# Two maxima of a head pair back to back in a two-layer decoder stage

## The reference, cut to what matters

```
def _mha(q_in, k_in, v_in, Wq, Wk, Wv, bv, causal):
    q, k = einsum(q_in, Wq), einsum(k_in, Wk)
    v = einsum(v_in, Wv) + bv
    scores = einsum('bhse,bhte->bhst', q, k) * HEAD ** -0.5     # 16 heads of 16
    if causal: scores = where(tril, scores, -inf)
    return einsum('bhst,bhte->bhse', softmax(scores), v)        # heads side by side
sa = _mha(x, x, x, Wq1, Wk1, Wv1, bv1, causal=True)
x = _layernorm(sa + x, g1, be1)
ca = _mha(x, enc, enc, Wq2, Wk2, Wv2, bv2, causal=False)
x = _layernorm(x + ca, g2, be2)
```

## Time and profile before

| what | value |
|---|---|
| median of 3 runs | 1558.11 us (1557.0 to 1561.98) |
| the profiled execution | 1571.12 us, its span 1569.4 us |
| mean granted TensorE clock | 0.859 |
| PE busy | 1153.9 us (74%) |
| VectorE busy | 975.9 us (62%) |
| ScalarE busy | 613.1 us (39%) |
| GpSimd busy | 463.6 us (30%) |

### The profile page before, as it was taken

One profiled execution on the slowest core, in us unless ns is written; L12 is line 12 of the kernel. 1 busy time (PEld: TensorE's weight loads), 2 busy tenths in 40 slices (PEclk: granted clock), 3 DMA queues, 4 the chain that ended last, 5 costly groups with the idle time before them and its releaser, 6 DMA issues. The chain is left out here.

```text
span 1569.4 us, 26159 instructions
## 1 busy us (share of the span) xinstructions
PE 1153.9 (74%) x9362; PEld 767.7 (49%) x9362; DVE 975.9 (62%) x2633; ACT 613.1 (39%) x1214; POOL 463.6 (30%) x616
## 2 busy tenths in 40 slices
PE   2687767777499710788888888820599997699998
PEld 1364444444278610677777777720254543345454
DVE  4645566777247530788888888834465652477776
ACT  1334455666355201566566656500154443000000
POOL 4234554323426644133333333355110100100000
PEclk9777898999789855899999999965586876799999
DMA  6323222322023234565666556245121210101000
GB/s 187 106 58 98 68 86 83 124 79 62 20 82 117 92 120 177 212 234 211 206 231 239 202 208 233 72 129 174 56 59 46 74 31 28 55 27 34 26 9 14
DMA packets 130245, 171.35 MB, mean 109 GB/s; under 512 B 13747, under 2 KB 104646, under 8 KB 127174
## 3 DMA queue, kind: packets, MB, share of 16 engines
q1 hardware_dynamic: 126534, 160.77, 31.3%
q0 software_dynamic: 3584, 8.92, 1.8%
HBM read 123.31 MB, written 46.14 MB: 108 GB/s over the span
## 5 line engine op out<-in xcount | busy, mean ns | idle before, releaser
L1972 PE MATMUL moe_ps_u<-moe_x_hl,moe_up_hl 128*128 128x256 f16 x1932 | 226.5, 276 | 68.8 <-DVE moe_up_hl L2048 42.6
L1972 PEld LDWEIGHTS moe_ps_u<-moe_x_hl,moe_up_hl 128*128 128x128 f16 x1932 | 184.5, 99 | 110.8 <-DVE moe_up_hl L2048 49.1
L2335 PE MATMUL mix_ps_e<-wr_hl,mix_u_hl 128*128 128x512 f16 x768 | 172.4, 380 | 0.0
L2092 POOL CAST moe_mid_hl<-moe_mid 128x256 f16<-128x256 f32 x161 | 71.8, 446 | 291.8 <-DVE moe_mid L2063 291.8
L2048 DVE SCALAR_TENSOR_TENSOR moe_up_hl<-moe_up_in,moe_up_hl 128x512 f16<-128x512 f32 x161 | 123.3, 799 | 54.4 <-ACT moe_up_hl L2021 54.4
L542 ACT ACTIVATE dec_probs<-dec_ps_t 128x768 f32<-128x768 f32 (+1 forms) x128 | 117.2, 917 | 83.3 <-PE dec_ps_t L444 83.1
L2447 DVE SCALAR_TENSOR_TENSOR mix_acc<-mix_ps_e,mix_shares,mix_acc 128x256 f32<-128x256 f32 x256 | 110.3, 477 | 39.0 <-PE mix_ps_e L2335 38.7
L1294 DVE TENSOR_REDUCE memory_neg_m<-memory_ps_s 128x2 f32<-128x512 f32 x128 | 84.8, 689 | 66.2 <-PE memory_ps_s L1071 63.5
L2021 ACT ACTIVATE moe_up_hl<-moe_up_in 128x512 f16<-128x512 f32 x161 | 99.2, 619 | 62.0 <-DMA moe_up_in<-in_moe_w 62.0
L431 PE MATMUL dec_ps_s<-dec_k_st,dec_q_st 48*128 48x256 f16 (+1 forms) x512 | 51.5, 281 | 90.6 <-DVE dec_neg_m L640 47.1
L2335 PEld LDWEIGHTS mix_ps_e<-wr_hl,mix_u_hl 128*128 128x128 f16 x768 | 74.8, 98 | 83.4 <-issue 1.1
(11 more groups left out here) (278 smaller groups left out, 2101.1 us busy)
## 6 DMA issues: line engine op xcount, KB each, us to landing
moe_up_in<-in_moe_w SPq DMA_DIRECT2D x23, 1792.0 KB, 7.6
moe_down_in<-in_moe_w SPq DMA_DIRECT2D x23, 896.0 KB, 4.7
moe_raw<-in_mix_wr SPq DMA_DIRECT2D x32, 256.0 KB, 7.7
dec_q_dram<-dec_q_hl SPq DMA_DIRECT2D x48, 128.0 KB, 2.0
dec_k_dram<-dec_k_hl SPq DMA_DIRECT2D x48, 128.0 KB, 2.0
dec_q_st<-dec_q_dram SPq DMA_DIRECT2D x64, 96.0 KB, 2.5
dec_k_st<-dec_k_dram SPq DMA_DIRECT2D x64, 96.0 KB, 2.6
xs<-zeros SPq DMA_DIRECT2D x8, 736.0 KB
```

What stands on the lines that cost most here:

```text
L1972: mm = nc.tensor.matmul(bank[:, m, :], up_hl[t.slot][:, w, m, dc, f * P:(f + 1) * P], x_hl[t.slot][:, x, dc, :], start=(dc == 0 and w == x ...
L2335: mm = nc.tensor.matmul(ps_e[fill % RING][:, :, :], u_hl[t.slot][:, r, dc, k * P:(k + 1) * P], wr_hl[:, m, dc, 2 * q:2 * q + 2, :], start= ...
```

## The change

Within an eighth VectorE does both maxima first and everything else behind them. Some other calls are moved by an eighth with it: the low part of QUERY from eighth 2 to 1, the low part of KEY from 3 to 2, the divisions from 3 and 7 to 2 and 6. No instruction is added or taken away, no wait is changed, and the loops of the other engines stay.

```
                 for t in STEPS:
                     nxt, new, old, older = t + 1, t + 2, t - 1, t - 2
                     for p in range(PAIRS):
+                        if within(nxt):
+                            maximum(nxt, 2 * p)
+                            maximum(nxt, 2 * p + 1)
+                        if p == 0 and within(new):
+                            rows_low(new)
+                        if p == 1 and within(new):
+                            projected_low(new, QUERY, q_hl)
                         if p == 2 and within(new):
-                            projected_low(new, QUERY, q_hl)
-                        if p in (3, 7) and within(old):
+                            projected_low(new, KEY, k_hl)
+                        if p in (2, 6) and within(old):
                             divide(old, p // 4)
                         if p == 1 and within(older):
                             statistics(older)
                         if p == 4 and within(older):
                             normalise(older)
-                        if within(nxt):
-                            maximum(nxt, 2 * p)
-                        if p == 0 and within(new):
-                            rows_low(new)
-                        if p == 3 and within(new):
-                            projected_low(new, KEY, k_hl)
-                        if within(nxt):
-                            maximum(nxt, 2 * p + 1)
```

## The result

| | before | after |
|---|---|---|
| median of 4 runs | 1557.55 us (1556.51 to 1561.98) | 1540.04 us (1532.74 to 1541.24) |
| the profiled execution, its span | 1571.12, 1569.4 us | 1541.24, 1539.5 us |
| mean granted clock | 0.859 | 0.874 |
| PE / VectorE busy | 1153.9 / 975.9 us | 1139.3 / 975.2 us |

The ratio is 0.9872, interval [0.9836, 0.9909]. The forecast of 1549.0 had the direction, and its range held the time, because case 2 had set the lower edge; the gain is about twice the 9.1 us of the sum (17.5 by the medians), and lies in the interval of case 2, which I had given 0.22.

A forecast was written before the change was run, and what follows sets the result against it. The prediction took the decoder stage to be held by handovers between engines, with no engine full. Its terms, -19.0 + 13.3 - 3.4 = -9.1 us, took the median from 1558.11 to 1549.0; its 8-in-10 range was 1539.5 to 1555.

The forecast's parts named there:

- case 2: Filled hole ahead of QUERY also keeps the clock up: half to all of 9.5 us more, 1539.5 to 1544.3; chance 0.22.
- the sum: Decoder schedule: -19.0 (head) + 13.3 (later division) - 3.4 (normalisation) = -9.1 us, with the clock's effect taken as zero.
- Eighths 0 and 1: Head of the decoder step: rows_low behind maximum 1 starts QUERY 1.36 us earlier, 19.0 us over 14 steps.
- case 4: No change to be told: scores 1, not rows_low, set QUERY's start, so the head gives less; 1557.2 us, chance 0.10.
- Eighths 2 and 3: Division behind KEY's low part loses its cover: scores 4 come 1.00 us later a step, 13.3 us lost in all.
- The statistics: Moved behind QUERY's low part, their 0.94 us on VectorE cost nothing, since later maxima wait for the division anyway.
- The normalisation: Moved behind maximum 9, its collision with GpSimd's context split is hidden in four steps: 3.4 us gained.
- Case 3: The normalisation still holds VectorE where it counts: 3.4 us less gain, 1552.4 us; chance 0.10.
- The clock: Granted clock in decoder steps 0 to 8: taken as zero, between 9.5 us gained at QUERY and falls of 2.13 each.
- if QUERY and VALUE take other times than now: Sign in the trace after that would show the forecast wrong: changed durations of these decoder projections.
- Case 5: Slower: new hole ahead of the first values drops the clock there and at VALUE; eight falls, 1566.0 us; chance 0.08.

The follow-up runs named there:

- e7_norm_back: Changed kernel with the normalisation put back ahead of maximum 8; 1555.25 us, ratio 0.9891 to the kernel before.
- e2_key_ahead: Kernel before with only the low part of KEY moved ahead of the first division; 1578.74 us, ratio 1.0140 to the kernel before.
- e1_head_only: Kernel before with only rows_low moved behind maximum 1; 1541.68 us, ratio 0.9823 to the kernel before.
- e4_hole_back: Changed kernel with one wait added: PE waits for rows_low ahead of scores 1; 1558.14 us, ratio 0.9989 to the kernel before.
- e6_swap: Changed kernel with the division ahead of the low part of KEY in eighth 2; 1547.94 us, ratio 0.9835 to the kernel before.

## Why the prediction was wrong in its size

**Eighths 0 and 1: right.** -1.36 forecast, -1.45 measured (3.51 to 2.06). The order is the one drawn: maximum 1, scores 1, rows_low, then QUERY. This also refutes case 4: QUERY waits for rows_low (0.55 us) and not for scores 1.

**Eighths 2 and 3: right.** +1.00 forecast, +0.91 measured (5.45 to 6.36). The product ends a little earlier, and the first values fit in as computed, from 288.98 to 290.05, under scores 4 at 290.17. PE's new wait ahead of them is 0.87 there.

**The statistics: right.** At 285.15, maxima 4 and 5 behind them, ended at 287.35, and the low part of KEY at 287.52 waits 0.17 for ScalarE.

**The normalisation: right in size, wrong in its cause.** Scores 4 to scores 5 take 1.72 us in a step where they took 2.60, in order of time:

```profile
139.59 0.34 PE L431 MATMUL dec_ps_s<-dec_k_st,dec_q_st 48*128 48x128 f16 x4 [0.25 <-DVE dec_neg_m L640]
...
140.37 1.16 POOL L743 TENSOR_TENSOR context<-dec_ctx_raw,context 128x512 f16<-128x512 f32 x1 [1.31 <-ACT context L533]
...
141.08 1.23 DVE L669 TENSOR_SCALAR dec_total<-dec_total,dec_mv,dec_rstd 128x256 f32<-128x256 f32 x2
141.31 0.50 PE L431 MATMUL dec_ps_s<-dec_k_st,dec_q_st 48*128 48x128 f16 x4 [0.84 <-DVE dec_neg_m L640]
```

The pair meets the end of the split (1.23 instead of 0.73), hidden. But e7_norm_back and e2_key_ahead are free of the collision with the normalisation at its old place: the later division shifts the split, a step that I had not followed as far as GpSimd. Case 3, in which the normalisation still costs its 3.4 us, fails with it.

**The schedule in sum: nearly right.** Re-measured it is 14 x 1.45 = 20.3 less, 13 x 0.91 + 0.2 = 12.0 more and 3.4 less: -11.7 where I had -9.1.

**The clock: the step that failed.** "In steps 0 to 8 the granted clock falls and rises ... I take zero." It was worth -8.6 at QUERY, against a bound of 9.5 that stood in the text. KEY gave back 0.3 (1.26 us above full clock instead of 0.94), and VALUE, which I feared for, gave 0.8 (5.6 instead of 6.4). With these the sum is -20.8, of the 22.5 by which this decoder ended earlier. The sign that the prediction itself had set, "if QUERY and VALUE take other times than now", was met. In the second pair of executions QUERY gives 7.7 and VALUE 0.2, and yet the decoder ends only 13.0 earlier; what took the rest there is open.

What shows the cause is e1_head_only, by one move, together with where the clock falls in all traces; e4_hole_back shows that one wait undoes the gain at QUERY, and leaves open how. What misled me was the argument against case 2: "the steps at full clock have the same hole of 2.3 us before scores 1 and no fall." (The hole is 2.09 there.) That a hole is met without a fall in some steps shows that it isn't enough by itself; it doesn't show that it isn't needed. With 2.04 to 2.09 us of idleness ahead of all nine QUERYs that were long, these should have weighed more than the steps without a fall. The two kinds of step also differ in what stands ahead: in steps 3 to 8 PE idled another 0.9 to 1.3 us ahead of the values that stand before the turned rows, in 9 to 13 it did not. No run tests that, and in the second execution of before QUERY was long in step 9, without it.

**Case 5: a true fall, too small.** e2_key_ahead shows what the move does alone: four VALUEs of the cross layer at 2.56 to 2.66, and a schedule of 13 x 0.91 + 0.2 - 3.4 = 8.6 us turned into 19.9. In the first execution of the changed kernel VALUE is long in steps 2 to 7 alone, five of which had it before (2 to 5 and 7); of the eight steps on which the case was built (8 to 13, 1 and 6) only 6 fell. In the second, 1, 6 and 12 did. The prediction's sentence on idle stretches speaks for cases 2 and 5, not 2 and 3 as it says.

The Trainium skill (TensorE: Matmul & The Clock Gate, section "HAM oscillation — how this bites in real kernels") has idle stretches between bursts as what drops the clock. The trace of the kernel before agrees, with the clock at 0.50 from 259.4 on, behind the hole that ended at 258.86, and QUERY at 2.77. e4_hole_back has QUERY at 2.77 too, but with the fall ahead of the hole that was put back. Which of the holes that are left decides at VALUE no run here shows.

Open are that question, what lets the clock fall ahead of the turned rows in e4_hole_back, and what of the difference between two executions of one kernel (396.5 and 405.1) is chance.

## What to carry to other kernels

Where matmuls of one shape show two durations, list each occurrence with the hole ahead of it, and price the durations as a term of the sum with its own sign: here the clock at QUERY gave 8.6 us beside the 11.7 of the order. A fall that is prevented at one place can come at another, so count the falls of the whole step. Where a wait is put back as a test, see in the trace whether the clock falls behind it or ahead of it. Between two operations on which PE waits, VectorE does nothing else; work that waits for a third engine goes to the tail of an eighth, behind the maxima, and a division stays beside a projection that covers it. Where other stages scatter by more than the change is worth, compare the end of the stage that was changed.

## What the runs showed of the hardware

A stage that no kernel here touches, the attention over memory, took 165.3 to 194.7 us from the first to the last of its shifted scores, in 13 executions with the same instructions. Stretches of it, in e2_key_ahead and in e6_swap, with the busy times of PE, weight loads, VectorE, ScalarE and GpSimd, the granted clock, DMA share and GB/s:

```profile
1150.00:1316.00 166.00, 152.33 (x1232) 81.68 (x1234) 101.12 (x207) 90.48 (x128) 12.91 (x18) 0.85 0.19 55
```

```profile
1108.00:1304.00 196.00, 182.01 (x1242) 93.95 (x1244) 101.97 (x207) 91.34 (x129) 13.01 (x19) 0.70 0.15 46
```

VectorE and ScalarE are busy for the same time in both; PE takes 29.7 us more at a granted clock of 0.70 instead of 0.85. So the same code on the same data lands on either side, by up to 29 us, and this is the largest part of the scatter of one per cent in the totals that I could place. The expert stage took 368.9 us, from the first to the last matmul of its second product, in both executions of the first pair.
